# Attention and a top-2 mixture of experts on one core: reciprocals four pairs later, statistics and top-2 moved, expert weights told in a second pass

## The reference

```python
def reference(x, ctx_2048, gate, w0, w1, wo):     # x, ctx: (32, 64, 256) f32
    x = x + xattn(layernorm(x), ctx, ctx)         # 8-row heads: over (32*8) blocks of 8 rows and 256 columns
    x = x + ffn(layernorm(x), gate, w0, w1, wo)
    return x

def xattn(q, k, v):        # after the reshape to (b*h, 8, 256)
    qk = einsum('bdm,bdn->bmn', qh, kh) / sqrt(8)
    sm = softmax(qk, axis=-1)
    return einsum('bmn,bcn->bcm', sm, vh)

def ffn(x, gate, w0, w1, wo):                     # 8 experts, 256 -> 512 -> 256
    weights, chosen = top_k(einsum('bsd,de->bse', x, gate), 2)
    combine = one_hot(chosen) weighted by softmax(weights)
    inter = silu(einsum('bsd,edm->bsem', x, w0)) * einsum('bsd,edm->bsem', x, w1)
    return einsum('bse,bsem,emd->bsd', combine, inter, wo)
```

## Time and profile before

| | |
|---|---|
| median of 3 runs | 544.45 us (544.16 to 548.63) |
| the profiled execution's own time | 544.45 us |
| its span | 542.7 us |
| busy in the span: TensorE matmul, VectorE, ScalarE, GpSimd | 439.4, 283.7, 230.6, 216.0 us |
| mean granted TensorE clock | 0.898 of 2.4 GHz |

### The profile page before, as it was taken

How to read it: one execution, slowest core, us unless ns; L and a number is a source line. 1 busy time by engine, 2 the same in 40 slices (tenths; PEclk the granted TensorE clock), 3 DMA queues, 4 the chain that set the end, 5 groups by cost and what they waited for, 6 DMA issues and landing times.

```text
span 542.7 us, 10122 instructions
## 1 busy us (share of the span) xinstructions
PE 439.4 (81%) x3150; PEld 228.9 (42%) x3151; DVE 283.7 (52%) x599; ACT 230.6 (42%) x456; POOL 216.0 (40%) x224
## 2 busy tenths in 40 slices
PE   0336789889897967999714899999999999999991
PEld 0301234234342423332312465665665665665660
DVE  7169887988888857964789122222222222222220
ACT  0302698686777764787400322222222222222220
POOL 3530703262626333333383134534444544544522
PEclk9955699898999997788955799999999999999996
DMA  5899547586776892537393022232232232232321
GB/s 183 200 302 280 167 118 197 168 229 185 217 211 187 245 276 92 200 103 248 109 383 105 30 40 39 42 54 39 40 56 39 42 55 39 41 56 39 41 38 19
DMA packets 45208, 69.91 MB, mean 129 GB/s; under 512 B 6887, under 2 KB 34200, under 8 KB 45176
## 3 DMA queue, kind: packets, MB, share of 16 engines
q1 hardware_dynamic: 29698, 41.37, 27.0%
q0 software_dynamic: 11424, 24.39, 19.8%
q10 hardware_dynamic: 4054, 3.72, 2.4%
HBM read 42.57 MB, written 26.58 MB: 127 GB/s over the span
## 4 chain that ended last, share of the span: by engine, by line
PE 53%; DMA 18%; DVE 13%; ACT 6%; SPq 6%; issue 2%; POOLq 0%; POOL 0%; DVEq 0%; ACTq 0%
PE max_ps L1379 25%; DMA den<-acc 7%; PE ring_ps L1389 6%; PE pv_ps L1389 6%; ACT pt L742 5%; PE pv_ps L1283 5%; DVE mx L888 5%; DMA acc<-pvs 4%; PE ring_ps L1362 3%; PE ring_ps L1266 3%; SPq L425 2%; DMA q_img<-qpart 2%; PE max_ps L1178 2%; PE ring_ps L1352 2%; SPq L371 2%
## 5 line engine op out<-in xcount | busy, mean ns | idle before, releaser
L888 DVE TENSOR_REDUCE mx<-max_ps 128x4 f32<-128x1024 f32 x128 | 150.3, 1216 | 29.8 <-PE max_ps L1178 29.5
L742 ACT ACTIVATE pt<-ring_ps 128x512 f32<-128x512 f32 x256 | 139.1, 598 | 48.5 <-PE ring_ps L1266 45.8
L1379 PE MATMUL max_ps<-w_sb,pt 128*128 x312 | 143.0, 602 | 0.9 <-ACT pt L813 0.9
L682 POOL DMA_INDIRECT out<-rb,sidx x39 | 62.1, 1591 | 119.3 <-DVE gidx L1126 55.4
L1150 DVE TENSOR_TENSOR pt<-pt,max_ps 128x512 f32<-128x512 f32 x39 | 26.8, 688 | 125.2 <-PE max_ps L1379 66.2
L1283 PE MATMUL pv_ps<-pt,w_sb 128*27 128x256 f32 (+2 forms) x1024 | 85.4, 419 | 1.4 <-ACT pt L742 0.6
L1178 PE MATMUL max_ps<-K,Q 48*128 48x256 bf16 x512 | 56.8, 306 | 33.1 <-DVE mx L888 24.7
L1379 PEld LDWEIGHTS max_ps<-w_sb,pt 128*128 128x128 f32 x312 | 57.2, 193 | 58.8 <-issue 58.8
L1266 PE MATMUL ring_ps<-Q,K 50*128 50x256 f16 x512 | 54.4, 294 | 14.2 <-ACT pt L742 12.9
L820 ACT ACTIVATE pt<-ring_ps 128x512 f32<-128x512 f32 x39 | 23.3, 597 | 71.5 <-PE ring_ps L1362 71.5
L674 POOL DMA_INDIRECT pt<-xrow,gidx x39 | 38.8, 996 | 28.5 <-issue 14.0
(11 more groups left out here) (161 smaller groups left out, 398.7 us busy)
## 6 DMA issues: line engine op xcount, KB each, us to landing
w_sb<-in_L_ffn_w_kernel POOLq DMA_DIRECT2D x16, 512.0 KB, 7.6
K<-k_img SPq DMA_DIRECT2D x16, 448.0 KB, 6.0
Q<-q_img SPq DMA_DIRECT2D x16, 448.0 KB, 7.2
q_img<-qpart SPq DMA_DIRECT2D x32, 192.0 KB, 3.9
k_img<-kpart SPq DMA_DIRECT2D x28, 192.0 KB, 3.8
wo_sb<-in_L_ffn_wo_kernel POOLq DMA_DIRECT2D x8, 512.0 KB, 9.2
acc<-pvs SPq DMA_DIRECT2D x7, 512.0 KB, 3.8
q_sb<-in_x SPq DMA_DIRECT2D x16, 128.0 KB, 4.8
```

What stands on the lines that cost most here:

```text
L682: g.indirect_dma_start(xacc, bass.IndirectOffsetOnAxis(ap=sidx[sl.par][:, 0:1], axis=0), y_sb[sl.par], None, compute_op=ALU.add).then_inc( ...
L742: a.activation(pt[:, (2 * i + h) % PTN, :, :], bank(key)[:, :, :], ACT.Exp, scale=SCALE).then_inc(ring_read, 1)
L888: v.tensor_reduce(mx[:, t % 2, :, :, p].rearrange("q mt h -> q h mt"), max_ps[n % 2][:, :, :, :], axis=AX.X, op=ALU.max).then_inc(max_read, 1)
L1379: last = nc.tensor.matmul(flat(max_ps[sl.par][:, bank_of]), lhsT=xT[sl.par][:, k * P:(k + 1) * P], rhs=weight(w, e, KC, k), start=(k == 0) ...
```

## The change

- SyncE loads all 16 tiles of x at once; VectorE takes the statistics of the last ten in the prologue, GpSimd their rsqrt before `split_q(1)`, and ScalarE normalises them before the first exponential, ahead of its issues for the rest of the context.
- `recip` moves from pair 2 to pair 6 of its tile and `rows_stats` from pair 4 to pair 7. SyncE, in odd tiles, issues `store_stack` and `store_rows` ahead of `store_rd` and `load_rb`; the last x rows are loaded two tiles earlier. GpSimd does `split_q` before `residual_norm`, and issues w0's loads and half of wo's in two groups of 4 and 8, in place of four groups of 2 loads and two more of 2.
- `choose` no longer runs in the loop: eight tiles go together behind it, then four, then the rest as before.
- The one-hot tables are both made by VectorE, with two products (token numbers) before the 32 matmuls. The four products for the weights, and what they need, follow behind the first gather's indices. 32 further matmuls (`slot_weights`) sum them between the first two experts. `onehot_s` lies in K[0] and the top-2 tables in K[2].

```diff
-            load_qk(1)
-            for t in range(6, 10):
-                sp.dma_start(q_sb[:, t, :], tile_of(x, t)).then_inc(x_in[t // 2], 16)
-            load_max(0)
-            for t in range(10, T):
+            for t in range(6, T):          # now right behind the first six loads
                 sp.dma_start(q_sb[:, t, :], tile_of(x, t)).then_inc(x_in[t // 2], 16)
...
-                    if t == T - 2:
+                    if t == T - 4:
                         sp.wait_ge(ring_full, slots["exp", PAIRS * (T - 4) - 1, 1] + 1)
                         sp.dma_start(x_last, x_rows[ST - 1]).then_inc(xl_in, 16)
                 else:
                     if t + 1 < T:
                         load_max(t + 1)
+                    if s + 3 < ST:
+                        store_stack(s + 3)
+                    if t >= 5:
+                        store_rows(s - 2)
                     if t >= 3:
                         store_rd(s - 1)
                         load_rb(s - 1)
-                    if t >= 5:
-                        store_rows(s - 2)
-                    if s + 3 < ST:
-                        store_stack(s + 3)
...
             split_k(1)
+            rsqrt(6, T, 4)
             split_q(1)
             split_k(2)
             split_q(2)
-            rsqrt(6, T, 4)
...
             for m in range(3):
                 residual_sum(m)
                 split_k(m + 5)
+                split_q(m + 5)
                 residual_norm(m)
-                split_q(m + 5)
             residual_sum(3)
-            load_w0(0)
-            load_w0(1)
             residual_norm(3)
-            load_w0(2)
-            load_w0(3)
             residual_sum(4)
-            load_w0(4)
-            load_w0(5)
+            for e in range(4):
+                load_w0(e)
             residual_norm(4)
-            load_w0(6)
-            load_w0(7)
+            for e in range(4, E):
+                load_w0(e)
+            for e in range(4, E):
+                load_wo(e)
             residual_sum(5)
-            load_wo(4)
-            load_wo(5)
             residual_norm(5)
-            load_wo(6)
-            load_wo(7)
...
+            a.wait_ge(nbias_done, 3)
+            for t in range(6, T):
+                normalise(t)
             a.wait_ge(qk_in[0], 64)
...
-                if 3 <= i < 3 + T - 6:
-                    a.wait_ge(nbias_done, 3)
-                    normalise(i + 3)
...
+            ln1_stats(6, T)
+            ln1_bias(6, T, 4)
...
-                if n == LEAD:
-                    ln1_stats(6, T)
-                if n == LEAD + 2:
-                    ln1_bias(6, T, 4)
-                if t >= 3 and t % 2 == 1 and p == 2:
+                if t >= 3 and t % 2 == 1 and p == 6:
                     recip((t - 3) // 2)
-                if t >= 4 and t % 2 == 0 and p == 4:
+                if t >= 4 and t % 2 == 0 and p == 7:
                     rows_stats((t - 4) // 2)
-                if t >= 6 and t % 2 == 0 and p == 2:
-                    choose((t - 6) // 2)
...
-            choose(ST - 4)
-            count(ST - 4, range(T - 6))
+            choose(ST - 5, range(T - 8))
+            count(1, range(T - 8))
             recip(ST - 2)
             residual_last(0)
             stats_last([x2_last[:, 0, :]], 2)
-            choose(ST - 3)
-            count(ST - 3, unit_tiles[ST - 3])
+            choose(ST - 3, range(T - 8, T - 4))
+            count(2, range(T - 8, T - 4))
...
-            where(1).then_inc(onehot_done, 1)
-            v.wait_ge(norm_done, 1)
-            then(v.tensor_scalar(wts[:, 0, :], norm[:, :], WSCALE, None, ALU.mult))
-            then(v.tensor_tensor(wts[:, 1, :], wts[:, 0, :], e2[:, :], ALU.mult))
-            then(v.tensor_copy(pay[:, 1], wts[:, :, :]))
-            v.tensor_tensor(pay[:, 2], wts[:, :, :], pay[:, 1], ALU.subtract).then_inc(pay_done, 1)
-            then(where(0))
-            tell(0)
-            v.wait_ge(pay_done, 1)
-            tell(1)
-            tell(2)
+            for k in range(TOPK):
+                then(v.tensor_tensor(onehot_t[:, k], ..., ALU.is_equal))
+            for k in range(TOPK):
+                then(tell(0, k))
...
+            v.wait_ge(norm_done, 1)          # behind the first gather's indices and spare_of
+            ...                               # wts and pay, as above
+            for k in range(TOPK):
+                for c in range(1, PAY):
+                    tell(c, k).then_inc(weights_done, 1)
...
+                if sl.peeled and sl.t == 1:
+                    v.wait_ge(weights_full, 1)
+                    then(v.tensor_copy(wlow[:, :], y_ps[1][:, 1, NT:2 * NT]))
+                    v.scalar_tensor_tensor(wslot[:, :], y_ps[1][:, 1, 0:NT], 1.0, wlow[:, :], op0=ALU.mult,
+                                           op1=ALU.add).then_inc(weights_read, 1)
...
+            def slot_weights():
+                pe.wait_ge(weights_done, TOPK * (PAY - 1))
+                for k in range(TOPK):
+                    for t in range(T):
+                        n = k * T + t
+                        last = nc.tensor.matmul(y_ps[1][:, 1, 0:(PAY - 1) * NT]...,
+                                                lhsT=onehot_s[:, k, t, :], rhs=told[:, 1:PAY, k, t, :], ...)
+                last.then_inc(weights_full, 1)
...
             def output(sl, e):
                 pe.wait_ge(interT_done, sl.t + 1)
+                if sl.peeled and sl.t == 1:
+                    pe.wait_ge(weights_read, 1)
...
                     turn_x(sl.at(1))
+                if sl.peeled and sl.t == 0:
+                    slot_weights()
                 if sl.has(-1):
                     output(sl.at(-1), e_before)
```

More of the change, by code:

```diff
@@ L56, in xattn_ffn_kernel @@
     tile_order = [t for tiles in unit_tiles for t in tiles]
-    top_before = [2 * sum(len(tiles) for tiles in unit_tiles[:n]) for n in range(UNITS)]
     slots = {}
@@ L658, in _ @@
             g.tensor_tensor(norm[:, :], norm[:, :], mone[:, :], ALU.pow).then_inc(norm_done, 1)
-            g.wait_ge(onehot_done, 1)
-            for c in range(PAY):
-                if c == 1:
-                    g.wait_ge(pay_done, 1)
-                g.tensor_tensor(told[:, c, 1], onehot_t[:, 1], pay[:, c, 1, :, None].broadcast_to([P, T, NT]),
-                                ALU.mult).then_inc(pool_told, 1)
             def gather(sl):
@@ L916, in rows_stats, with choose @@
                 v.tensor_scalar(veps2[:, :], mv2[:, 0:2, 1], EPS, None, ALU.add).then_inc(veps2_done, 1)
[L918 to L921 removed]
+            tops = [0]
+            def choose(m, tiles):
+                a0, a1 = tiles[0], tiles[-1] + 1
                 v.wait_ge(ring_read, slots["logits", m] + 1)
[L923 to L931 removed]
+                for t in tiles:
+                    v.max(top[:, t, :], lgs[:, t, :]).then_inc(top_chain, 1)
+                tops[0] += len(tiles)
+                v.wait_ge(top_chain, tops[0])
+                v.tensor_tensor(gap[:, a0:a1], top[:, a0:a1, 1], top[:, a0:a1, 0], ALU.subtract).then_inc(gap_done, 1)
+                for t in tiles:
+                    v.max_index(topi[:, t, :], top[:, t, :], lgs[:, t, :]).then_inc(top_chain, 1)
+                tops[0] += len(tiles)
+                v.wait_ge(top_chain, tops[0])
+                v.tensor_copy(chosen[:, :, a0:a1], topi[:, a0:a1, 0:TOPK].rearrange("p u k -> p k u")).then_inc(top_done, 1)
             def recip(s):
@@ L964, in count @@
             def count(m, tiles):
-                v.wait_ge(top_done, m + 1)
+                v.wait_ge(top_done, m)
                 a, n = tiles[0], len(tiles)
@@ L1334, in _ @@
                     pe.wait_ge(told_done, n + 1)
-                    if n == T:
-                        pe.wait_ge(pool_told, PAY)
-                    last = nc.tensor.matmul(pv_ps.rearrange("p u m -> p (u m)")[:, 0:PAY * NT]
-                                            .rearrange("p (c i) -> p c i", c=PAY),
-                                            lhsT=onehot_s[:, k, t, :], rhs=told[:, :, k, t, :],
+                    last = nc.tensor.matmul(pv_ps[:, 0, 0:NT], lhsT=onehot_s[:, k, t, :], rhs=told[:, 0, k, t, :],
                                             start=(n == 0), stop=(n == TOPK * T - 1))
@@ L1364, in turn_inter @@
                 last.then_inc(inter_turned, 1)
+            def slot_weights():
[3 more added lines that the diff above has]
+                        n = k * T + t
+                        last = nc.tensor.matmul(y_ps[1][:, 1, 0:(PAY - 1) * NT].rearrange("p (c i) -> p c i", c=PAY - 1),
+                                                lhsT=onehot_s[:, k, t, :], rhs=told[:, 1:PAY, k, t, :],
+                                                start=(n == 0), stop=(n == TOPK * T - 1))
+                last.then_inc(weights_full, 1)
             def expert(sl):
```

72 lines of the change are left out of this document (29 added, 43 removed).

## The result

The changed kernel took 521.98 us (median of 4 runs, 518.74 to 527.99), the kernel before 546.54 us beside it: a ratio of 0.953, 95% interval 0.945 to 0.961. (Ratios leave out single runs over 1.5% above the fastest of their kernel, here the one of 527.99 us.) Forecast were 524.6 us, 514 to 536. The profiled execution took 521.89 us, its span 520.1 us for 542.7.

What follows compares the result with a forecast made beforehand. It took attention to be bound by stops, mainly VectorE's reciprocal waiting for the denominators (23.1 us). Terms +1.6 - 4.3 - 1.8 - 5.1 - 8.9 - 0.2 - 4.3 + 3.15 = -19.85 us took 544.45 to 524.6 us, range 514 to 536.

Steps and rivals of the forecast that it cites:

- Part 1: Start through tile 2: ten tiles' statistics and normalisations moved into the prologue, forecast -4.5 us in all.
- +1.6: Start: the extra loads of x make the first images land later, up to 2.4 us; 1.6 taken.
- -4.3 and -1.8: Early tiles: statistics leave VectorE's queue, 4.3 us (2.3 to 6); normalisations leave ScalarE's, 1.8 us (0 to 4).
- Tiles 3 to 10: Attention: reciprocal's waits vanish, SyncE's queue becomes the bound at 24.6 us per two tiles; gain 5.1 us (0 to 12.0).
- rival B: Attention: SyncE's queue does not bind, 22.9 us per two tiles, no stops in tiles 11 to 13; 516.2 us, chance 0.24.
- Tiles 11 to 13: Late attention: gain 8.9 us (5 to 11.4), with 1.5 us kept for stops from 4 MB of weight loads.
- rival C: Attention: stops return as waits for transfers, 25.9 us per two tiles, last reciprocal 4 us late; 537.8 us, chance 0.18.
- To the gather: Last evacuation to first gather: slot tables 4.3 us shorter, top-2 and last reciprocal -0.2 us together; forecast -4.5.
- "+1.2": Behind attention: last reciprocal 1.2 us late (0 to 5) through rows_stats and six more tiles of top-2.
- The second pass: Between the first two experts: 32 more matmuls and a later output(0) cost 3.15 us (1.9 to 6).
- Rival E: First experts: 32 matmuls at the low clock (5.3 us) and the wait eat the 4.3 us; 527.4 us, chance within forecast's 0.52.
- The shared port: Behind the first gather: VectorE's four products could hold up GpSimd's second gather by 0.8 us; sum left unchanged.

Runs made afterwards that it cites:

- e5: Kernel before with only x's loads, statistics and normalisations in the prologue: 539.43 us, ratio 0.992.
- e2: Changed kernel with the reciprocal and rows_stats back at pairs 2 and 4: 536.43 us, ratio 0.979 to the kernel before.
- e4: Kernel before with only the later reciprocal and statistics (pairs 6 and 7), SyncE's order as it was: 551.48 us, ratio 1.013.
- e6: Changed kernel with SyncE's old order in odd tiles (rd, rb, rows, then stack stores): 533.52 us, ratio 0.978 to the kernel before.
- e8: Changed kernel without tile 13's eight weight loads, experts 4 to 7 using expert 3's weights (output not the reference's): 517.67 us, ratio 0.952 to the kernel before.
- e9: Changed kernel with the same eight weight loads issued behind the landing of the last rb: 519.85 us, ratio 0.957 to the kernel before.
- e14: Changed kernel with the twelve early weight loads in fours: tile 0, end of tile 11, behind the last rb: 516.31 us, ratio 0.948 to the kernel before.
- e11: Changed kernel with the 32 matmuls of the weights' second pass issued twice; one run, read from its profile alone: experts 248.69 us.
- e13: Changed kernel with GpSimd's split_q put back behind residual_norm: 522.18 us, ratio 0.960 to the kernel before.
- e10: Changed kernel with the twelve early weight loads in fours: tile 0, end of tile 11, tile 13: 519.09 us, ratio 0.953 to the kernel before.

## Why the prediction was right

**Part 1** was larger than its terms: -7.0 for -4.5. The loads of x cost nothing for +1.6; the first scores came no later (30.58 us for 30.86). The rest, -5.8 and -1.2, lies within the bounds given for the -4.3 and -1.8 taken, and e5, -5.6 us in all, shows that it is kept to the end.

**Tiles 3 to 10**, -6.5 for -5.1, in the range of the term. That the reciprocal's waits vanish was right. That SyncE's queue would be the bound was not: rows_stats was not seen waiting for x2 in these tiles. In the changed kernel acc was there 3.0 to 3.3 us after its issue for the 4.5 taken, and rd let rb go after 2.8 to 3.6 for the 4.0 taken. With these the forecast's own sum of a turn is about 23 us, rival B's, where 24.3 were measured; what holds these tiles now stays open. And the step treated the later reciprocal as the gain and SyncE's new order as its price. The square of e2, e4 and e6 shows that neither is worth anything alone. That top-2 out of the loop is worth nothing was not tried by itself.

**Tiles 11 to 13** is the term that was mis-sized. I saw the 4 MB, put them beside den, rd and rb, and kept 1.5 us for them. They cost tile 13 8 to 9 (against e8, e9, e14), and the transfer that mattered most was not on my list: the rows of the maxima, two loads of 8 KB. On the other side tiles 11 and 12 gained 11.5 for 8.9 + 1.5, just above the upper bound of that term: tile 12 took 10.16 us, less than the 11.25 that the forecast took as the length of a tile without a stop. Taken together, -2.3 against -8.9: the one place where rival C, stops that come back as waits for transfers, was right.

The rule quoted from the Trainium skill (DMA: Bandwidth & Descriptors, Queues, rings and completion order), that an increment lands only after earlier writes of its engine across queues, pointed here, and I had applied it to the stack stores. There it cost nothing that can be seen: rd behind eight stores let rb go after 3.6 us (93.74 to 97.32). For the weights no run proves it: in the changed kernel only one weight load of 512 KB was issued ahead of the second small one, and in e11 the two were issued at the same time (205.98 + 0.68 and 206.72 us), yet TensorE went on only 12.9 and 13.8 us after the first issue.

**To the gather**, -6.5 for -4.5. The tables gave -4.3 as worked out. The last reciprocal no longer waits, and VectorE's division behind the last evacuation comes 2.93 us after it, before 5.05; the "+1.2" was a loss that did not come.

**The second pass**, +0.1 for +3.15, is the other step that failed. By the rows it is 1.32 us less the 0.6 taken off, 0.7 us; the +0.1 is within the spread of that stretch. Half of the miss is the price of a matmul: I scaled the 32 told matmuls (5.32 us), but those wait for VectorE's comparisons one by one; alone they go every 36 to 41 ns (1.32 us for 32, 1.16 for 32 more), where by the Trainium skill's figure (TensorE: Matmul & The Clock Gate, Back-to-back issue gap) of about 81 ns a pair, stated for 128 columns, the 32 would take an estimated 2.6 us; these have 78 columns. The other half is a misreading of the code: the wait for VectorE's sums belongs to the second output, which starts 4.7 us after the sums have been read. Rival E fell with it.

**The shared port.** By the Trainium skill's rule (SBUF — State Buffer, SBUF: two separate sides), that GpSimd can't write descriptors while VectorE runs an operation in a two-port mode, the second gather could have been held up by an estimated 0.8 us. Its issue took 0.97 us beside VectorE's four products (274.33 us), the first one, just before, 1.10: no hold-up is seen in this trace. Whether VectorE's products here are such operations, no run shows.

So the forecast was right in its direction and its main mechanism (stops behind the denominators). That its total came within 3 us was luck: four gains taken 1.1 to 2.5 us too small, and a loss of 3 that did not come, made up for one of 9 that I had put at 1.5.

## What to carry to other kernels

In this kernel bulk loads cost nothing that could be seen where nobody waited for a small one, and 5 to 9 us where somebody did; so look for the stretches in which the DMA engines are idle and no short round trip is under way, and put the weights there, rather than at the places where the issuing engine happens to be free. List every small transfer that is waited for in the stretch, the ones that never waited so far above all. When a wait is moved later in one engine's order, move the work that stood behind it in the issuing queue ahead of it in the same edit: alone, either half may be a loss.

## What the runs showed of the hardware

- Two loads of 8 KB took 12.9 us from their first issue to their use when 4 MB were issued 0.47 us behind it, 13.8 with 0.74 us between (e11), 6.5 with 0.93 (e13), and 8.8 when 2 MB were issued 0.36 us ahead (e10). The round trip of rd in tile 13 took 1.5, 1.9 and 3.6 us without the weights (e9, e8, e14), 7.6 and 11.4 us beside the 4 MB (e13, changed).
- After a stop of 7.28 us TensorE ran at a granted clock of 0.50 (1.2 GHz) for some 10 us: eight products with V took 1.07 us in place of 0.64. Stop and tail together made tile 13 9.1 us longer than before.
- 32 accumulating matmuls of 128x78, float16, ran in 1.32 us, 64 in 2.48, at the higher clock (granted 1.00 in those stretches).
